# A transformer block on one core: less for GpSimd at three seams, dummy transposes in TensorE's first block, and keys doubled in halves

## The chip, the cores and the metric

The kernel runs on one core of one Trainium2 chip. The metric is the device time of one execution in microseconds. The engines are TensorE (PE), VectorE (DVE), ScalarE (ACT), GpSimd (POOL) and SyncE (SP, which only issues DMAs here). Each works through its own queue in order and waits for others by semaphores.

## The reference

```
x = x + 0.5 * ffn(layernorm(x))            # mixture of 8 experts, 2 chosen per row, and a shared one
x = x + attention_block(layernorm(x))      # attention of 16 heads of 64, Wo, residual, then an MLP
x = x + 0.5 * ffn(layernorm(x))            # the same ffn and weights again
# x: 4 x 1024 x 256, float32
# ffn: scores = sigmoid(x @ gate_W) * route_scale; top 2, weights divided by their sum
#      h_e = gelu(x @ W1_e + b1_e); y_e = h_e @ W2_e + b2_e; sum of gate_e * y_e, plus the shared expert
# attention: q = (ln(x)*s_q + b_q) @ Wq + bq, likewise k and v; p = softmax(q k' / 16 + mask)
```

## The kernel before, in words

The 4096 rows are worked in 8 blocks of 512 (`NB`), the feature dimension of 256 in 2 chunks (`DC`). Every product is split: a float32 operand becomes a rounded high part (mostly ScalarE, names with `_hi`) and a low part that is the difference (mostly VectorE, `_lo`), and three matmuls (`PARTS`) are summed.

`ffn_phase` is built twice; the first time `tail` is true. It prepares weights first: ScalarE rounds the gate weights, w1, w2, b2 and the selection matrix `sel`; VectorE makes the low part of w1, GpSimd that of w2 (L570). Then `over_blocks` runs `body` for each block. In a body the loop variable `e` goes over 9 experts, the shared one first. For each, TensorE computes the hidden layer (`first_layer`, L840) and broadcasts the gate (`gate`, L858), ScalarE applies gelu (L458), VectorE multiplies by the gate (L673), ScalarE rounds (L450), VectorE takes the low part (`lo`, L679), and TensorE adds the second layer two experts behind (`second_layer`, L879). Between these stand, at fixed values of `e`, the steps that prepare the next block: statistics, normalisation, transposes (L807), logits (L817), and the gates (`neg_logits`, `choices`, `gates`), whose transposed form `gst` (`gate_stack`, L668) is what the gate matmuls of the next block need. GpSimd computes powers (reciprocal roots and the exponential of the logits); ScalarE does the exponential in the first block alone.

With `tail`, the body also normalises the finished rows of the block before (`z_stats`, `z_norm`, `zz_stats`, `zn_norm`, transposes to zT), for attention. In blocks 0 and 7 it splits the scaled QKV weights (`qkv_hi`, `qkv_lo`, at the places of `QKV_AT`). The bias of the layer norm has to go through the QKV weights too: for the first `AT_ONCE` groups of 128 columns of Q and K by `first_bias` (L891), for the rest by products and a sum on GpSimd in the last block (`bias_products`, L545 and L548) and matmuls against ones in attention's first four steps (`later_bias`, L905).

`attention_phase` takes two heads at a time ("pair") for 1024 rows; one step `k` is 128 rows of queries of one head: scores (L1538), maximum (L1453), exponential (L1305), division on GpSimd (L1378), eight transposes (L1550), copies, and values (L1574). Before step 0, `FIRST` lists five projections: K, K, Q, Q, V. ScalarE copies each out of PSUM with its bias (`stage`, L1267), GpSimd rounds both heads (`heads_hi`, L1352 and L1353), VectorE takes the low parts (L1428). Each head's K is then copied to the other 64 partitions by DMA (`double_k`, L1152), which the scores of step 0 wait for. The last block's z chain (`rest["z_stats"]` and so on) is worked between these and the first seven steps. The MLP and the second `ffn_phase` follow; the change does not touch what they do.

Of the kernel before, what the change touches and what calls it, by code (L numbers as in the profile page):

```python
# [20 lines left out]
F32 = mybir.dt.float32  # L21
# [103 lines left out]
def ffn_phase(nc, turns, tag, src, dst, w, tail):  # L125
# [8 lines left out]
    AT_ONCE = 2  # L134
# [99 lines left out]
    if tail:  # L234
        names += " gate_in w1_in w2_in zeroed gw_hi w1_hi w2_hi sel gw_lo w1_lo w2_lo b2_hi b2_stack kept"
        names += " z_veps z_bn z_stats z_rs z_rstd z zn zT_ps zT_hi zT_lo zT_out z_out qkv_in v_in summed qs qkv_hi qkv_lo qkv_out bias_ps bias"
    else:
        names += " w1_back w2_back"
# [17 lines left out]


# [10 lines left out]
    def on_sync(sp):  # L268

        def first_loads():  # L270
# [8 lines left out]
            for at, to in ((0, E), (E, 2 * E + 1), (LOW, LOW + NE)):  # L279
                sp.dma_start(b2_in[at:to], w["b2"][0:to - at]).then_inc(s["w2_in"], 16)  # L280
            sp.dma_start(sel_in[:], w["sel"]).then_inc(s["w2_in"], 16)
# [11 lines left out]
        def keep_weights():  # L293
# [4 lines left out]
            sp.wait_ge(s["w2_lo"], 1)  # L298
# [98 lines left out]
    def on_scalar(act):  # L397
# [29 lines left out]

        def xt_hi(i, par):
# [23 lines left out]
        def body(i, par, first, last):  # L452
            for e in range(NE):
# [10 lines left out]
                if e == 2 and not last:  # L464
# [37 lines left out]
    def on_gpsimd(pool):  # L502
# [38 lines left out]
        def bias_products(k):  # L541

            pool.wait_ge(s["qkv_lo"], (k + 1) * DC)
            for c in range(DC):
                o = pool.tensor_scalar(qkv_in[:, k, c], qkv_in[:, k, c], ln[:, k, c, 1:2], 1.0, ALU.mult, ALU.mult)  # L545
            o.then_inc(s["summed"], 1)
            pool.wait_ge(s["summed"], 2 * k + 1)
            pool.tensor_tensor(qkv_in[:, k, 0], qkv_in[:, k, 0], qkv_in[:, k, 1], ALU.add).then_inc(s["summed"], 1)  # L548

        def body(i, par, first, last):  # L550
            if tail and last:
                bias_products(0)
                bias_products(1)
# [8 lines left out]
            if tail and last:  # L562
                bias_products(2)
                pool.wait_ge(s["summed"], 6)
        if tail:
# [3 lines left out]
            pool.wait_ge(s["w2_hi"], 1)  # L569
            pool.tensor_tensor(w2p[:, 1], w2_in[:], w2p[:, 0].bitcast(F32), ALU.subtract).then_inc(s["w2_lo"], 1)  # L570
# [5 lines left out]
    def on_vector(dve):  # L576
# [129 lines left out]

        def zt_lo(i, c, ps):
# [17 lines left out]
        if tail:  # L725
# [12 lines left out]
            gates(0)  # L738
            dve.wait_ge(s["b2_hi"], 1)
# [1377 lines left out]
```

## Time and profile before

| | us |
|---|---|
| median of 3 runs (lowest to highest) | 2468.53 (2466.96 to 2470.21) |
| profiled execution | 2464.61 |
| its span | 2462.8 |
| PE busy in the span | 2404.3 |
| DVE busy | 1866.7 |
| ACT busy | 1680.8 |
| POOL busy | 1529.1 |

The span is the time between the first and the last instruction that the profiler saw; busy PE time counts matmuls in flight and is not PE at its peak. The mean granted clock of TensorE is 0.994 of full speed: only a few short stretches are at half. The chain that ended last is on PE for 81% of the span and on DVE for 8%.

### The profile page before, as it was taken

Reading aid. Unit: us, or ns where it says so; the run is one execution under the profiler, and the core shown is the slowest. Engines: PE = TensorE matmul, PEld = TensorE weight load, DVE = VectorE, ACT = ScalarE, POOL = GpSimd, SP = SyncE. Lnnn points to the kernel's source line nnn. Section 1 sums busy time; section 2 is a strip of 40 time slices with the busy share of each in tenths; the row PEclk is TensorE's granted clock in tenths of the full one; section 3 lists DMA queues with packets and bytes.
Section 4 is the critical chain, followed back from the end, with each engine's and each line's share of the span. In section 5 each row is a group of like instructions: output and inputs, shape, how many; then the busy total and the mean of one; then the engine's idle time right before and its main releaser. Section 6 shows DMA issues by size and latency. Waiting matters only on the chain.

```text
span 2462.8 us, 46531 instructions
## 1 busy us (share of the span) xinstructions
PE 2404.3 (98%) x14504; PEld 2086.9 (85%) x14504; DVE 1866.7 (76%) x3594; ACT 1680.8 (68%) x2913; POOL 1529.1 (62%) x1550
## 2 busy tenths in 40 slices
PE   7999799999999999999999999999999999999999
PEld 6988688888888888888888888888888889988888
DVE  6777777878878787887878878787887865556665
ACT  4554477878778787887878778787787864443333
POOL 2333477777777777777777777777777755542220
PEclk9999999999999999999999999999999999999999
DMA  4522531213222122221213212122221345331111
GB/s 175 199 102 94 171 116 47 87 57 97 72 65 94 43 85 77 85 94 43 85 60 94 84 53 94 43 85 83 79 94 43 108 167 172 119 128 35 48 51 43
DMA packets 127894, 220.15 MB, mean 89 GB/s; under 512 B 6778, under 2 KB 89620, under 8 KB 118932
## 3 DMA queue, kind: packets, MB, share of 16 engines
q1 hardware_dynamic: 127764, 218.78, 27.5%
q8 instruction: 37, 0.61, 0.1%
q14 instruction: 93, 0.76, 0.1%
HBM read 114.95 MB, written 53.48 MB: 68 GB/s over the span
## 4 chain that ended last, share of the span: by engine, by line
PE 81%; DVE 8%; issue 6%; POOL 2%; ACT 2%; DMA 0%; DVEq 0%; SPq 0%; ACTq 0%; POOLq 0%
PE a_ov L1574 19%; PE a_sc L1538 18%; PE a_tr L1550 18%; PE a_pj L1493 7%; PE a_pj L1502 4%; PE g_acc L879 3%; PE g_hid L840 3%; PE f_acc L879 2%; PE f_hid L840 2%; PE m_proj L1976 2%; PE m_hid L2042 1%; DVE f_hp L679 1%; POOL m_zin L1828 1%; PE m_acc L2013 1%; PE f_aux L817 1%
## 5 line engine op out<-in xcount | busy, mean ns | idle before, releaser
L1453 DVE TENSOR_REDUCE a_nmax<-a_sc 128x1 f32<-128x1024 f32 x512 | 626.8, 1224 | 262.4 <-PE a_sc L1538 254.0
L1378 POOL TENSOR_SCALAR a_pr<-a_pr,a_rden 128x1024 f32<-128x1024 f32 x512 | 576.2, 1126 | 258.8 <-DVE a_rden L1458 189.6
L1299 ACT ACTIVATE a_pT<-a_tr 128x512 fp32r<-128x512 f32 x1024 | 559.9, 596 | 209.1 <-PE a_tr L1550 207.6
L1464 DVE TENSOR_TENSOR a_pT<-a_tr,a_pT 128x512 fp32r<-128x512 f32 x1024 | 650.1, 677 | 15.6 <-ACT a_pT L1299 15.6
L1574 PE MATMUL a_ov<-a_pT,a_v_s 128*128 128x512 f32 x2048 | 600.2, 415 | 3.1 <-DVE a_half L1444 2.0
L1305 ACT ACTIVATE a_pr<-a_sc,a_nmax 128x1024 f32<-128x1024 f32 x512 | 573.4, 1120 | 32.5 <-DVE a_nmax L1453 28.9
L1538 PE MATMUL a_sc<-a_k_s,a_q_s 128*128 128x512 f32 x2048 | 555.2, 393 | 6.7 <-DMA a_k_s<-a_k_s 6.7
L1550 PEld LDWEIGHTS a_tr<-f_ident,a_pr 128*128 128x128 f32 x4096 | 473.9, 140 | 89.5 <-DVE a_pT L1464 17.8
L1550 PE MATMUL a_tr<-f_ident,a_pr 128*128 128x128 f32 x4096 | 537.6, 273 | 6.9 <-DVE a_pT L1464 6.9
L1538 PEld LDWEIGHTS a_sc<-a_k_s,a_q_s 128*128 128x128 f32 x2048 | 380.5, 188 | 87.3 <-DMA a_k_s<-a_k_s 6.9
L1574 PEld LDWEIGHTS a_ov<-a_pT,a_v_s 128*128 128x128 f32 x2048 | 347.5, 189 | 54.2 <-issue 4.9
L1493 PE MATMUL a_pj<-a_z_s,a_wqk_s 128*128 128x512 f32 x756 | 193.7, 391 | 2.2 <-issue 2.2
L1493 PEld LDWEIGHTS a_pj<-a_z_s,a_wqk_s 128*128 128x128 f32 x756 | 141.7, 188 | 34.5 <-issue 2.6
L1267 ACT ACTIVATE a_staged<-a_pj,f_bias 128x512 f32<-128x512 f32 x126 | 86.7, 688 | 91.1 <-PE a_pj L1493 68.9
L458 ACT ACTIVATE g_act_out<-g_hid,f_b 128x512 f32<-128x512 f32 x72 | 49.6, 688 | 144.7 <-PE g_hid L840 144.7
L458 ACT ACTIVATE f_act_out<-f_hid,f_b 128x512 f32<-128x512 f32 x72 | 49.3, 684 | 114.9 <-PE f_hid L840 114.9
L879 PEld LDWEIGHTS f_acc<-f_w2p,f_hp 128*128 128x128 f32 x864 | 113.1, 192 | 10.5 <-DVE f_hp L679 5.7
L879 PE MATMUL f_acc<-f_w2p,f_hp 128*128 128x256 f32 x864 | 116.7, 285 | 3.2 <-DVE f_hp L679 2.5
L879 PEld LDWEIGHTS g_acc<-g_w2p,g_hp 128*128 128x128 f32 x864 | 112.1, 191 | 8.4 <-DVE g_hp L679 3.3
L840 PE MATMUL f_hid<-f_xT,f_w1p 128*128 128x512 f32 x432 | 118.6, 412 | 0.0
L879 PE MATMUL g_acc<-g_w2p,g_hp 128*128 128x256 f32 x864 | 115.7, 284 | 1.3 <-DVE g_hp L679 0.9
L840 PE MATMUL g_hid<-g_xT,g_w1p 128*128 128x512 f32 x432 | 113.1, 397 | 0.0
(214 smaller groups left out, 3273.8 us busy)
## 6 DMA issues: line engine op xcount, KB each, us to landing
a_z_s<-zT SPq DMA_DIRECT2D x32, 1024.0 KB, 7.9
a_k_s<-a_k_s SPq DMA_DIRECT2D x64, 512.0 KB, 5.9
a_wqk_s<-w_split SPq DMA_DIRECT2D x64, 256.0 KB, 3.2
a_v_s<-a_v_b SPq DMA_DIRECT2D x16, 1024.0 KB, 4.6
att<-a_ao SPq DMA_DIRECT2D x32, 512.0 KB, 2.9
m_in<-att SPq DMA_DIRECT2D x16, 1024.0 KB, 6.0
a_wv_s<-w_split SPq DMA_DIRECT2D x17, 512.0 KB, 3.8
zT<-f_zT SPq DMA_DIRECT2D x8, 1024.0 KB, 3.9
```

What stands on the lines that cost most here:

```text
L458: act.activation(act_out[:, e % 3], hid[:, (par + e) % 2], ACT.Gelu, bias=b1[:, weights_of(e):weights_of(e) + 1]).then_inc(s["gelu"], 1)
L840: o = pe.matmul(hid[:, (par + e) % 2], w1p[:, a, (c * NE + x) * HID:(c * NE + x + 1) * HID], xT[:, par, c, b], start=(n == 0), stop=(n == 5))
L879: o = pe.matmul(acc[:, t], hp[:, e % 3, a, t * P:(t + 1) * P], w2p[:, b, x * D:(x + 1) * D], start=False, stop=(e == NE - 1 and (a, b) == ...
L1299: act.activation(pT[:, (u // 4) % 2, 0, 4 * part:4 * part + 4, (u % 4) * P:(u % 4 + 1) * P], tr[:, part].rearrange("p (t q) -> p t q", t=4 ...
L1305: act.activation(pr[:, k % NP], sc[:, k % 2], ACT.Exp, bias=nmax[:, k % NP:k % NP + 1], accum_out=den[:, k % NP:k % NP + 1]).then_inc(s["e ...
L1378: pool.tensor_scalar(pr[:, k % NP], pr[:, k % NP], rden[:, k % NP:k % NP + 1], 1.0, ALU.mult, ALU.mult).then_inc(s["normed"], 1)
L1453: dve.tensor_reduce(nmax[:, k % NP:k % NP + 1], sc[:, k % 2], AX.X, ALU.max, negate=True).then_inc(s["negmax"], 1)
L1464: dve.tensor_tensor(to[:, 1], tr[:, part].rearrange("p (t q) -> p t q", t=4), to[:, 0].bitcast(F32), ALU.subtract).then_inc(s["tr_lo"], 1)
L1493: o = pe.matmul(bank[:], wqk_s[:, "QK".index(kind), c, a], z_s[:, c * 2 + b, part], start=(i == 0), stop=(i == 5))
L1538: o = pe.matmul(sc[:, k % 2, kb * BT:(kb + 1) * BT], q_s[:, slot, head, tile * P:(tile + 1) * P], k_s[:, slot, head, a, kb * BT:(kb + 1) * ...
L1550: o = pe.transpose(tr[:, part, j * P:(j + 1) * P], pr[:, (k - LAG) % NP, (4 * part + j) * P:(4 * part + j + 1) * P], ident[:])
L1574: o = pe.matmul(ov[:], v_s[:, vslot, kt, 2 * vhead:2 * vhead + 2] .rearrange("p k f -> p (k f)"), pT[:, blk % 2, a, kt], start=(kt == 0 an ...
```

## The change

- In the first block (`tail` and `first`), TensorE does dummy transposes of the identity into `acc`, which is overwritten later: 20 before the first transposes, 22 after them, 6 after the logits, 10 after `first_bias` and 10 after `gates_up`.
- GpSimd no longer makes w2's low part. VectorE does (`w2_low`), the shared expert's columns at e = 0 and the others at e = 1 of block 0. Its first residual `lo(0, 0)` moves ahead of the loop.
- b2 and sel get a semaphore of their own, and ScalarE rounds them before w2.
- In block 0 the steps that prepare block 1 come two experts later (`later`), `choices` one later.
- `AT_ONCE` goes from 2 to 1.
- GpSimd's bias products and sums go; in the last block, at e = 4, 6 and 7, ScalarE scales one chunk (`bias_product`) and VectorE multiplies and adds (`bias_sum`).
- In attention's five first projections ScalarE writes the second head's high part straight from PSUM, GpSimd only the first head's. K is doubled in two halves, ahead of the stores of zT and of rows on SP. The z chain of the last block starts at steps 1 to 3 instead of before the fourth projection.

The diff, cut to its core:

```diff
-    AT_ONCE = 2
+    AT_ONCE = 1
+    SUMS_AT = {4: 0, 6: 1, 7: 2}
+    def later(first):
+        return 2 if tail and first else 0
...
+        def bias_product(k):
+            act.wait_ge(s["qkv_lo"], (k + 1) * DC)
+            act.activation(qkv_in[:, k, 1], qkv_in[:, k, 1], ACT.Identity, scale=ln[:, k, 1, 1:2]).then_inc(s["scaled"], 1)
...
-                if e == 2 and not last:
+                if e == 2 + later(first) and not last:
                     xt_hi(i + 1, 1 - par)
...
+                if tail and last and e in SUMS_AT:
+                    bias_product(SUMS_AT[e])
...
-            act.wait_ge(s["w2_in"], 80)
-            act.activation(w2p[:, 0], w2_in[:], ACT.Identity).then_inc(s["w2_hi"], 1)
+            act.wait_ge(s["sel_in"], 64)
             act.activation(b2s[:], b2_in[:], ACT.Identity).then_inc(s["b2_hi"], 1)
             act.activation(sel[:], sel_in[:], ACT.Identity).then_inc(s["sel"], 1)
+            act.wait_ge(s["w2_in"], 16)
+            act.activation(w2p[:, 0], w2_in[:], ACT.Identity).then_inc(s["w2_hi"], 1)
             act.wait_ge(s["neg"], 1)
             act.activation(nl[:], nl[:], ACT.Exp).then_inc(s["expneg"], 1)
...
-            if tail and last:
-                bias_products(0)
-                bias_products(1)
...
-            if tail and last:
-                bias_products(2)
-                pool.wait_ge(s["summed"], 6)
...
-            pool.wait_ge(s["w2_hi"], 1)
-            pool.tensor_tensor(w2p[:, 1], w2_in[:], w2p[:, 0].bitcast(F32), ALU.subtract).then_inc(s["w2_lo"], 1)
...
+        def bias_sum(k):
+            dve.wait_ge(s["scaled"], k + 1)
+            dve.scalar_tensor_tensor(out=qkv_in[:, k, 0], in0=qkv_in[:, k, 0], scalar=ln[:, k, 0, 1:2], in1=qkv_in[:, k, 1],
+                                     op0=ALU.mult, op1=ALU.add).then_inc(s["summed"], 1)
+        def w2_low(which):
+            dve.wait_ge(s["w2_hi"], 1)
+            dve.tensor_tensor(w2p[:, 1, which], w2_in[:, which], w2p[:, 0, which].bitcast(F32), ALU.subtract)\
+                .then_inc(s["w2_lo"], 1)
...
             gates(0)
+            lo(0, 0)
...
+                    w2_low(slice((NE - 1) * D, NE * D))
+                if tail and first and e == 1:
+                    w2_low(slice(0, (NE - 1) * D))
                 if not last:
-                    if e == 0:
+                    if e == 0 + later(first):
                         x_stats(i + 1, 1 - par)
...
-                    if e == 7:
+                    if e == 7 + later(first) // 2:
                         choices(i + 1)
...
+        def keep_warm(n):
+            for t in range(n):
+                pe.transpose(acc[:, t % 2, 0:P], ident[:], ident[:])
...
                         first_bias()
+                        keep_warm(10)
                     gates_up(i)
+                    if tail:
+                        keep_warm(10)
...
             pe.wait_ge(s["gate_in"], 64)
+            keep_warm(20)
             transposes(0, xn, s["xn"], s["xT_ps"])
+            keep_warm(22)
             pe.wait_ge(s["gw_lo"], 1)
             logits(0, 0)
+            keep_warm(6)
...
+        for part in range(2):
+            sp.wait_ge(s["first_split"], part + 1)
+            double_first(part)
         rest["store_zT_ahead"]()
         rest["store_rows"]()
-        sp.wait_ge(s["first_split"], 2)
-        double_k(0)
...
+        def second_head_hi(kind, part, n):
+            _, hi, _ = parts_of(kind, part, n % 2, 0)
+            act.activation(hi[1], bank_of(n, True)[rows_of_head(1)], ACT.Identity, bias=bias_of(rows_of_head(1), 0, "QK".index(kind)))\
+                .then_inc(s["head1_hi"], 1)
         for n, (kind, part) in enumerate(FIRST):
             stage(kind, n, n % 2, 0, True)
+            if kind != "V":
+                second_head_hi(kind, part, n)
...
-                if first and k == 1:
+                if first and k == 2:
                     rest["z_norm"]()
...
-                heads_hi(kind, part, n, n % 2, 0, n)
+                (x0, _), hi, _ = parts_of(kind, part, n % 2, 0)
+                pool.wait_ge(s["staged"], n + 1)
+                pool.tensor_scalar(hi[0], x0, 1.0, 1.0, ALU.mult, ALU.mult).then_inc(s["head0_hi"], 1)
...
-                if first and k in (0, 3):
+                if first and k in (1, 3):
                     rest["z_rstds"](k // 3)
...
-            if n == 3:
-                rest["z_stats"]()
...
+                if first and k == 1:
+                    rest["z_stats"]()
-                if first and k == 2:
+                if first and k == 3:
                     rest["zz_stats"]()
```

## Rows read from the trace of the kernel before

**Rows 1.** The page's head.
```profile
span 2462.8 us, 46531 instructions
```

**Rows 2.** Chain of waits, 0 to 110 us: start us, us, what.
```profile
13.46 3.56 PE f_aux L817 x16
...
17.83 3.55 DVE f_sg L630
...
26.84 0.70 DVE f_gst L668
...
28.38 2.56 PE f_hid L840 x6
...
42.56 1.39 PE f_hid L840 x6
...
58.74 1.28 DVE f_qkv_s L703
```

**Rows 3.** Timeline, 0 to 72 us: start us, us, engine, line, operation, [idle before <-releaser].
```profile
6.01 0.22 ACT L482 ACTIVATE f_gwp<-f_gw_in 128x16 fp32r<-128x16 f32 x1 [3.87 <-DMA f_rsc<-in_rscale]
...
10.01 1.94 PE L807 MATMUL f_aux<-f_ident,f_xn 128*128 128x128 f32 x8 [10.01 <-DVE f_xn L597]
...
14.04 2.12 ACT L488 ACTIVATE f_w2p<-f_w_in 128x2304 fp32r<-128x2304 f32 x1 [1.46 <-DMA f_w_in<-in_w]
...
16.25 5.09 POOL L570 TENSOR_TENSOR f_w2p<-f_w_in,f_w2p 128x2304 fp32r<-128x2304 f32 x1 [7.80 <-ACT f_w2p L488]
...
60.53 0.68 DVE L668 CAST f_gst<-f_aux 128x512 fp32r<-128x512 f32 x1
```

**Rows 4.** Timeline, 212 to 275 us.
```profile
222.98 0.68 DVE L668 CAST f_gst<-f_aux 128x512 fp32r<-128x512 f32 x1
...
254.88 2.34 POOL L548 TENSOR_TENSOR f_qkv_in<-f_qkv_in 128x1024 f32<-128x1024 f32 x1
254.91 2.35 DVE L653 TENSOR_TENSOR f_ga<-f_iota,f_idf 128x32 f32<-128x32 f32 x1
...
259.19 1.12 PE L827 MATMUL f_aux<-f_ident,f_gpad 128*128 128x128 f32 x4 [4.73 <-DVE f_zT L709]
...
260.35 0.69 DVE L668 CAST f_gst<-f_aux 128x512 fp32r<-128x512 f32 x1
```

**Rows 5.** Windows: us, busy (instructions) of each engine, PEclk, DMA share, GB/s.
```profile
26.00:28.00 2.00, 1.22 (x5) 0.81 (x4) 1.18 (x6) 0.00 (x0) 0.00 (x0) 0.50 0.00 0
...
2188.00:2189.00 1.00, 1.00 (x11) 1.00 (x10) 0.24 (x1) 0.87 (x2) 0.00 (x0) 1.00 0.00 0
...
2193.00:2194.00 1.00, 1.00 (x4) 0.79 (x3) 0.65 (x1) 0.11 (x1) 1.00 (x1) 0.53 0.00 0
```

**Rows 6.** Timeline of the last block, 253 to 285 us.
```profile
254.00 1.14 ACT L425 ACTIVATE f_qkv_s<-f_qkv_in,f_ln 128x1024 fp32r<-128x1024 f32 x1
...
277.00 2.08 ACT L401 ACTIVATE f_zz<-f_res,f_zshift,f_zrs 128x256 f32<-128x256 f32 x4 [2.32 <-POOL f_zshift L534]
...
281.03 1.70 PE L879 MATMUL f_acc<-f_w2p,f_hp 128*128 128x256 f32 x12 [1.28 <-DVE f_hp L679]
```

**Rows 7.** Timeline of the step into attention, 275 to 345 us.
```profile
297.55 1.12 POOL L1353 TENSOR_SCALAR a_k_s<-a_staged 64x512 fp32r<-64x512 f32 x1
...
308.67 2.08 PE L1538 MATMUL a_sc<-a_k_s,a_q_s 128*128 128x512 f32 x4 [6.68 <-DMA a_k_s<-a_k_s]
...
312.78 1.17 PE L905 MATMUL a_ov<-f_iota,f_qkv_in 128*128 128x1 f32 x10
```

**Rows 8.** Chain of waits, 225 to 372 us.
```profile
302.41 6.22 DMA a_k_s<-a_k_s
```

**Rows 9.** The page's DMA issues: KB each, us to landing.
```profile
a_wqk_s<-w_split SPq DMA_DIRECT2D x64, 256.0 KB, 3.2
```

**Rows 10.** TensorE's timeline, 2176 to 2216 us.
```profile
2188.37 1.04 PE L2027 MATMUL m_hT_ps<-f_ident,m_hn 128*128 128x128 f32 x8
2190.11 1.95 PE L817 MATMUL g_aux<-f_gwp,g_xT 128*128 128x16 f32 x16 [0.70 <-DVE g_xT L604]
```

More of the change, by code:

```diff
@@ L279, in first_loads @@
             for at, to in ((0, E), (E, 2 * E + 1), (LOW, LOW + NE)):
[L280 to L281 removed]
+                sp.dma_start(b2_in[at:to], w["b2"][0:to - at]).then_inc(s["sel_in"], 16)
+            sp.dma_start(sel_in[:], w["sel"]).then_inc(s["sel_in"], 16)
             sp.dma_start(w2_in[:], w["w2"]).then_inc(s["w2_in"], 16)
@@ L757, in body @@
                     result(i - 1)
-                if e > 0:
+                if e > 0 and not (tail and first and e == 1):
                     lo(i, e - 1)
-                elif not first:
+                elif e == 0 and not first:
                     lo(i - 1, NE - 1)
@@ L794, in body @@
                         qkv_lo(k, c)
+                if tail and last and e in SUMS_AT:
+                    bias_sum(SUMS_AT[e])
         over_blocks(dve, body)
@@ L874, in second_layer @@
                               start=(t % 2 == 0), stop=False, skip_group_check=True)
+            if first and tail and e == 1:
+                pe.wait_ge(s["w2_lo"], 2)
             pe.wait_ge(s["h_lo"], i * NE + e + 1)
@@ L898, in later_bias @@
             if part == 0:
-                pe.wait_ge(s["summed"], 6)
+                pe.wait_ge(s["summed"], 3)
             ones = iota[:, 1:2]
             groups = [(k, g) for k, a, b in LATER_BIAS for g in range(a, b)]
-            n = len(groups) // parts
-            for at in range(part * n, part * n + n):
+            n = -(-len(groups) // parts)
+            for at in range(part * n, min(part * n + n, len(groups))):
                 k, g = groups[at]
@@ L926, in body @@
                 if not last:
-                    if e == 2:
+                    if e == 2 + later(first):
                         transposes(i + 1, xn, s["xn"], s["xT_ps"])
-                    if e == 3:
+                    if e == 3 + later(first):
                         logits(i + 1, 1 - par)
@@ L1153, in double_k, with double_first @@
                     .then_inc(s["k_dup"], 16)
+        def double_first(part):
+            cols = slice(part * BT, part * BT + BT)
+            for head, (a, b) in enumerate(((0, HD), (HD, 0))):
+                sp.dma_start(k_s[b:b + HD, 0, head, :, cols].bitcast(F32), k_s[a:a + HD, 0, head, :, cols].bitcast(F32))\
+                    .then_inc(s["k_dup"], 16)
         def move_v():
@@ L1285, in body @@
                         act.wait_ge(f["z_out"], NB * 16 + 16)
-                        act.wait_ge(f["bias"], 4)
                     if blk % 4 == 0 and not first:
@@ L1308, in body @@
                         kind, _, n, slot = piece_at(it, k)
+                        if first and k == 5:
+                            act.wait_ge(f["bias"], 4)
                         stage(kind, n, slot, (2 * it + 1 + k // STEPS) % PAIRS, False)
```

26 lines of the change are left out of this document (11 added, 15 removed).

## The prediction

> **What bounds the kernel now.** I read the page's head first: the span is 2462.8 us of the profiled execution's 2464.61 [rows 1], so 1.8 us lie outside it; TensorE is busy in nearly all of it, and the attention loop that fills most of it is not touched. So only the pauses in the first 345 us can move the time. I then read the chain of waits there and the timelines beside it. In the first block the chain goes through TensorE's 16 small logits matmuls (3.56 us), then VectorE's gate work, where one 128x32 operation takes 3.55 us [rows 2]. The timeline shows GpSimd's residual of w2 from 16.25 to 21.34, and the slow operation ends just after it [rows 3]; the same kind of operation elsewhere is over in 0.2 us, so some 3.4 us are GpSimd in VectorE's way. In the last block VectorE's copy of the gates (f_gst) comes 37.37 us after that of the block before, where the five intervals ahead took 32.49 each ((222.98-60.53)/5) [rows 3, 4]: 4.9 us late. There a 128x32 operation took 2.35 us beside GpSimd's sum over the bias products, and TensorE stood 4.73 us [rows 4]. Third, attention starts only after a pause of 6.68 us, in which the doubled K is copied by DMA [rows 7, 8].
>
> **The first block.** Removed: GpSimd's w2 residual. VectorE does it in two pieces, after the gates. That takes 3.4 us off VectorE's chain ahead of f_gst.
> Added on TensorE: 20+22+6 dummy transposes around the first transposes and logits, 10+10 around the first gates_up. Their price depends on the clock. Eight transposes take 1.94 us in the first block [rows 3] and 1.04 us at 2188.37 [rows 10]; less the tail of the last one (0.42 and 0.27) that is 0.22 us each at the low level (1.2 GHz) and 0.11 us at the high one (2.4 GHz). Six 512-column matmuls take 2.56 us low and 1.39 us high [rows 2]; the granted clock is 0.50 at 26 to 28 us and 1.00 at 2188 [rows 5].
> The first 20 can begin when the small loads are in (6.01, where ScalarE begins) and take 4.4 us low: to 10.4, where the real transposes began at 10.01 [rows 3]. That is 0 to 0.4 us late; ScalarE is rounding w1 then, so I take 0. If dummies raise the clock as dense work does, it is high by about 12 us. The 22 then end near 14.2 where the logits began at 13.46: 0.7 us late, but the logits themselves take about 1.8 instead of 3.56 (16 x 0.11 with a tail). The negated logits come 1.0 us earlier. ScalarE has finished rounding w2 at 16.16 (14.04+2.12) [rows 3], just before they are there, so its exponential does not wait. The words of the change put this exponential ahead of two roundings; in the diff it stays behind all of them, and only b2 and sel go ahead of w2, in the idle time before w2 lands. Worth 0 either way.
> Without the 3.4 us stall the gates are ready 4.4 us earlier (21.3). TensorE gets there at 16.6 (logits, 6 dummies) + 2.8 (12 matmuls) + 0.9 (bias, 8 instructions instead of 16) + 1.1 (10 dummies) = 21.4: level. f_gst is then at 23.1 instead of 27.5; it is late by one residual (0.7) and the b2 one (0.4), which now stand before it on VectorE. So 4.4 - 0.7 + the 0.6 that gates_up is faster at the high clock: about 4.4 us at this point (26.84+0.70 [rows 2]).
> Then the block's own order. w2's second piece is 2048 of 2304 columns, about 2.3 us on VectorE; stats, norm, transposes and logits of the next block come two experts later, choices one later and directly ahead of the gates. TensorE first runs ahead of before by two experts (6.1 us), and gives it back at the end: choices start when the last expert's residual is done (49.0), then 2.2 + 2.2 + two qkv residuals of 1.28 [rows 2] + 1.3 put f_gst of the next block at 57.1 to its end, where it was 61.2 [rows 3]. What is late next is thus VectorE, not TensorE. Gain carried on: **4.0 us**, bounds 2.5 and 6.
>
> **The last block.** GpSimd's products and sums are gone, so f_gst comes at the usual interval: +4.9 us. The clock also does not fall behind a 4.73 us pause, where matmuls were half as fast for some 5 us; on the way to the first second-layer group I read 2.0 us from that. Together **+6.9**; bounds 5.5 and 7.5.
> In their place come three ScalarE scalings (1.14 each by its 128x1024 activation [rows 6]) and three VectorE multiply-adds (1.28 each by the qkv residual [rows 2]), at experts 4, 6 and 7. The one at expert 4 stands on ScalarE behind the normalisation of z, which waited for GpSimd until 277.00 and ran 2.08 [rows 6]. The multiply-add is at the head of VectorE's queue and waits for it: 279.1 + 1.14 + 1.3 = 281.6, and behind it stand gating and residual of two experts, 0.7 + 0.7, so TensorE's group that began at 281.03 after 1.28 us of waiting [rows 6] begins at 283.0: 1.9 late. At expert 7 the same pattern behind the second normalisation adds another 0.5, although the stalls by GpSimd there are gone. **-2.4**; bounds -0.5 (if another order of arrivals hides two) and -4. The pause before that group becomes 3.2 us. The pauses of 4.73 and 6.68 us brought the low clock [rows 4, 7]: the four score matmuls behind the second took 2.08 us; I take one fall in most executions, for three to four us at half speed: **-1.3**, bounds 0 and -2.
>
> **Into attention.** Each K and Q piece had both heads' high parts made by GpSimd, 1.12 us for one while VectorE works [rows 7]. Now ScalarE makes one straight from PSUM (in its idle time) and GpSimd the other. VectorE no longer waits for the second; K's two halves are split at about 298.8 and 300.7 (each step 0.7 on each of the two engines), where before the last issue of the copy was only out at 302.41 [rows 8]; each half is doubled as soon as it is split, ahead of two stores on the sync queue. The transfer after the last issue took 6.22 us for 512 KB [rows 8]; 256 KB pieces of the same queue take 3.2 in the median [rows 9]. From an issue at 301.3, with 3.2 to 5 us: 304.6 to 306.3, I take 305.6, against 308.67 [rows 7]: +3.0. The pause shrinks to about 3.6 us and the clock may still fall; before, the low level reached 3.6 us into the work, and now it could reach further: -0.7. Two more bias groups are made here, 4 instructions at 0.117 (1.17 per 10 [rows 7]): -0.5. The stats of z go from ahead of the last Q piece to step 1, the rest of that chain one step later; VectorE has 2 us gaps in these steps, ScalarE's 2.08 us normalisation now stands before the first transposed probabilities: 0, bounds -1.5 and +1.5. **+1.8** in all, bounds -0.5 and +5.
>
> **Sum.** 4.0 + 6.9 - 2.4 - 1.3 + 1.8 = 9.0 us. Against the profiled 2464.61 that is 2455.6; that execution lay 3.9 below the median of 2468.53, so for the median I say **2459.5**.
>
> **The rivals.**
> *Dummies that don't wake the clock.* For: no stretch of this trace is filled by transposes and followed by a rise; and a busy TensorE is not enough, since at 2193 the clock fell with no longer pause than 0.7 us behind it, after 16-column matmuls [rows 5, 10]. Against: the transposes just before those [rows 10] were passed with the clock at 1.00, which then stood for four more us [rows 5]. The price: the 22 low take 4.9 us from 12.3, so the logits end at 20.8; 6 dummies, 12 matmuls at 0.45, the bias and 10 dummies at 0.11 to 0.22 put gates_up at 29.3 to 31.5, and behind it 10 more: the first gate matmul is 3.5 to 7.5 us later than before (27.5). The block's own order takes the same 0.4 as above and a low stretch behind it 1. The first block then loses 5 to 8.8 instead of winning 4.0. Total 0.0 on the mild end (2468.5) and, if the clock stays low through the whole first stage, 3.8 us slower: **2472**. It decides at the 22 dummies ahead of the logits: the clock must be high before about 14 us.
> The Trainium skill says in "TensorE: Matmul & The Clock Gate", Part 4, PE-mode transpose, that transposes do not engage the full clock because they don't count as busy in the same way; that is this rival. By that rule the time would be the 2468.5 to 2472 just worked out, and by the rows of eight transposes passed at full clock it would be mine.
> *The last block keeps nothing.* ScalarE and VectorE queues are in order, and three waits are put at VectorE's head. If these cost the 4 us of the bound and a fall of the clock with each of two pauses (another 2), the sum is 9.0 - 1.6 - 2 = 5.4: **2463**. For it: at expert 4 ScalarE has 4.5 us of work (gelu and rounding 1.3, the normalisation 2.08, the scaling 1.14), and a block leaves 32.49 / 9 = 3.6 per expert.
> *Everything on the good side.* No fall of the clock at either seam and attention's ramp a step faster: 9.0 + 1.3 + 2.5 = 12.8: **2455.7**. Shorter pauses than those that brought a fall speak for it.
> *The words, not the deed.* The keys' copy may be bound by its start-up, not its size, so that halving gives nothing and only the 1 us earlier split counts: -2 of the sum, **2461.5**; within my range.
>
> **How the numbers follow.** My forecast 0.42, the good side 0.17, the last block 0.13, the unhalved copy 0.10, the sleeping clock 0.18 (two thirds of it near 2468, one third slower). The range to hold 8 in 10: from 2452 (between the good case and its bounds) to 2468. About 0.2% (5 us) is what a measurement of this kernel can tell: faster than 2463.6 is all of the first three but half of the last-block case, and the copy: 0.74; the sleeping clock and the rest within: 0.20; beyond 2473.5, its far end or a wait I haven't seen: 0.06.
>
> **What would show it.** The granted clock high before 14 us and no low stretch at 25 to 32 us; VectorE's L630 operation of the first block at 0.2 us; first f_gst near 23, second near 56.5, then equal intervals of 32.5 through the last block; a TensorE wait of about 3 us at expert 4 of the last block, released by VectorE behind the multiply-add; the first scores about 3 us after V's projection. It is wrong if the logits of the first block start at 17, or if the gains at the seams come back as waits on ScalarE in attention's first seven steps.

## The result: 0.2 to 0.4% faster, in executions of two kinds

The changed kernel was timed twice, each time beside the kernel before on the same chip.

| | changed, us | before, us | ratio, 95% interval |
|---|---|---|---|
| first, 8 executions | 2456.37 (2454.3 to 2464.42) | 2468.80 | 0.9957 [0.9947, 0.9967] |
| again, 11 executions | 2462.39 (2455.01 to 2465.5) | 2467.23 | 0.9980 [0.9971, 0.9990] |
| all 19 | median 2460.97 | | |

The two intervals do not meet. The reason lies in the executions: 8 of the 19 had a mean TensorE clock of 0.996 or more and a median of 2456.1 us, the other 11 lay below that (0.992 to 0.994) and had 2462.9, from 2459.4 to 2465.5. The first time there were six of the quick sort and two of the other, the second time two and nine. Of 81 executions of the kernel before, timed beside the second timing and the experiments, only one had a mean clock of 0.996; their median is 2467.1. So the change gains 11 us in one sort of execution and 4 in the other. One execution of each sort has a trace. Below, the two traces differ by one stretch of low clock where attention begins; of the other executions only time and mean clock are known.

### The profile after, of a quick execution

It took 2457.1 us with this span (page's head); before it was 2464.61 with [rows 1]:

```profile
span 2454.2 us, 46643 instructions
```

The timeline (start us, us, engine, line, operation, [idle before <-releaser]):

```profile
9.86 1.04 PE L822 MATMUL f_aux<-f_ident,f_xn 128*128 128x128 f32 x8
10.73 2.56 PE L904 MATMUL f_acc<-f_ident 128*128 128x128 f32 x22
13.45 1.92 PE L832 MATMUL f_aux<-f_gwp,f_xT 128*128 128x16 f32 x16 [0.15 <-DVE f_xT L601]
...
16.75 0.18 DVE L627 TENSOR_SCALAR f_sg<-f_nl 128x32 f32<-128x32 f32 x1 [0.66 <-ACT f_nl L506]
...
22.27 0.69 DVE L665 CAST f_gst<-f_aux 128x512 fp32r<-128x512 f32 x1
...
52.78 0.66 PE L842 MATMUL f_aux<-f_ident,f_gpad 128*128 128x128 f32 x4 [1.99 <-DVE f_gpad L661]
...
55.63 0.68 DVE L665 CAST f_gst<-f_aux 128x512 fp32r<-128x512 f32 x1
...
89.73 0.68 DVE L665 CAST f_gst<-f_aux 128x512 fp32r<-128x512 f32 x1
...
252.19 0.68 DVE L665 CAST f_gst<-f_aux 128x512 fp32r<-128x512 f32 x1
...
266.22 2.08 ACT L407 ACTIVATE f_zz<-f_res,f_zshift,f_zrs 128x256 f32<-128x256 f32 x4 [2.01 <-POOL f_zshift L548]
268.20 1.13 ACT L437 ACTIVATE f_qkv_in<-f_qkv_in,f_ln 128x1024 f32<-128x1024 f32 x1
269.37 1.28 DVE L707 SCALAR_TENSOR_TENSOR f_qkv_in<-f_qkv_in,f_ln 128x1024 f32<-128x1024 f32 x1 [4.36 <-ACT f_qkv_in L437]
271.91 2.38 PE L896 MATMUL f_acc<-f_w2p,f_hp 128*128 128x256 f32 x12 [2.63 <-DVE f_hp L676]
...
283.35 3.50 PE L896 MATMUL f_acc<-f_w2p,f_hp 128*128 128x256 f32 x24 [1.24 <-DVE f_hp L676]
...
286.69 1.55 PE L1541 MATMUL a_pj<-a_z_s,a_wqk_s 128*128 128x512 f32 x6
293.23 1.66 PE L1550 MATMUL a_pj<-a_wv_s,a_z_s 128*128 128x256 f32 x12 [0.27 <-ACT a_q_s L1309]
298.27 1.19 PE L1586 MATMUL a_sc<-a_k_s,a_q_s 128*128 128x512 f32 x4 [3.38 <-DMA a_k_s<-a_k_s]
...
313.74 1.40 DVE L576 BATCH_NORM_STATS2 f_zst<-f_zz 128x6 f32<-128x256 f32 x4
...
317.58 1.16 PE L1598 MATMUL a_tr<-f_ident,a_pr 128*128 128x128 f32 x8 [2.12 <-DVE a_pT L1509]
...
327.55 1.16 PE L1622 MATMUL a_ov<-a_pT,a_v_s 128*128 128x512 f32 x4 [0.63 <-DVE f_zT L718]
```

What to see, from the top. Eight transposes take 1.04 us, not the 1.94 of [rows 3], although nothing but twenty dummy transposes (5.61 to 10.0) stands ahead of them, and the logits take 1.92, not the 3.56 of [rows 2]. L627, the operation that took 3.55 in [rows 2], takes 0.18. The gates' copy (f_gst) comes at 22.27. In the last block it comes at the usual interval; the pause of [4.73] in [rows 4] is gone, and [2.63] at 271.91 is the new one, at the end of the row of waits ScalarE L407, ScalarE L437, VectorE L707. A second one, of 1.24, stands at 283.35. The pause before the scores is 3.38, where [rows 7] had 6.68. Behind it, at 317.58, TensorE waits 2.12 for VectorE.

The windows (us, busy and instructions of PE, PEld, DVE, ACT, POOL, then PEclk, DMA share, GB/s) show the two low stretches of that trace before attention (54 to 61 and 272 to 276), one behind each of the pauses of 1.99 and 2.63. That attention begins at 1.00 is what sets this execution apart from the slower one traced below:

```profile
55.00:60.00 5.00, 3.84 (x15) 3.40 (x15) 3.64 (x12) 1.21 (x2) 1.26 (x2) 0.50 0.87 367
...
273.00:276.00 3.00, 3.00 (x12) 2.61 (x11) 2.84 (x8) 0.02 (x1) 1.95 (x3) 0.50 1.00 356
...
300.00:305.00 5.00, 5.00 (x42) 4.83 (x41) 2.69 (x5) 2.24 (x4) 0.95 (x3) 1.00 0.69 185
```

And the last copy of K in the chain of waits, against [rows 8]:

```profile
293.76 4.46 DMA a_k_s<-a_k_s
```

### The profile page after: what moved, and what is told of

Same layout as the page of the kernel before. It is cut to its first block, busy times and chain, and to the rows that moved or that the text cites. A ratio compares the mean times of both kernels' runs of the same rounds, so it can differ in the third digit from the quotient of the medians.

```text
span 2454.2 us, 46643 instructions
## 1 busy us (share of the span) xinstructions
PE 2405.0 (98%) x14568; PEld 2087.9 (85%) x14568; DVE 1862.3 (76%) x3599; ACT 1686.6 (69%) x2920; POOL 1505.2 (61%) x1536
## 4 chain that ended last, share of the span: by engine, by line
PE 81%; DVE 8%; issue 6%; POOL 2%; ACT 2%; DMA 1%; SPq 0%; DVEq 0%; ACTq 0%; POOLq 0%
PE a_ov L1622 19%; PE a_sc L1586 18%; PE a_tr L1598 18%; PE a_pj L1541 7%; PE a_pj L1550 4%; PE g_acc L896 3%; PE g_hid L855 3%; PE f_acc L896 3%; PE f_hid L855 2%; PE m_proj L2025 1%; POOL m_zin L1877 1%; PE m_hid L2091 1%; DVE f_hp L676 1%; DVE g_hp L676 1%; PE g_aux L832 1%
```

## The experiments

Each has 5 to 12 executions; "quick" are those with a mean clock of 0.996 or more. They ran on three chips, each beside the kernel before, and the ratio is against that: e1 to e4 (2467.15 for before), e6 to e9 (2466.58), and e5, e10, e11 with the second timing of the changed kernel (2467.23). So only those last three ran on the same chip as the second timing of the changed kernel; whether a chip shifts the share of quick executions was not tested.

| kernel | median us | ratio, interval | quick: n, median | others: n, median |
|---|---|---|---|---|
| changed (both times) | 2460.97 | see above | 8, 2456.1 | 11, 2462.9 |
| e1 no dummies | 2464.24 | 0.9995 [0.9986, 1.0003] | 2, 2458.6 | 10, 2465.1 |
| e7 first 48 only | 2462.75 | 0.9985 [0.9975, 0.9995] | 2, 2455.7 | 9, 2464.3 |
| e9 before + dummies | 2466.44 | 1.0005 [0.9995, 1.0015] | 1, 2464.0 | 10, 2466.8 |
| e2 sums on GpSimd | 2462.46 | 0.9983 [0.9972, 0.9994] | 6, 2459.1 | 6, 2467.7 |
| e3 old seam | 2462.20 | 0.9983 [0.9971, 0.9994] | 1, 2458.1 | 10, 2463.1 |
| e11 one copy | 2462.37 | 0.9976 [0.9968, 0.9985] | 2, 2459.2 | 9, 2463.5 |
| e5 exponential first | 2459.25 | 0.9967 [0.9955, 0.9980] | 4, 2457.9 | 2, 2464.2 |
| e6 pauses filled | 2457.83 | 0.9974 [0.9964, 0.9985] | 8, 2457.0 | 4, 2464.1 |
| e4 scalings first | 2457.88 | 0.9965 [0.9952, 0.9978] | 2, 2453.1 | 3, 2459.5 |
| e8 = e4 + e6 | 2458.52 | 0.9967 [0.9954, 0.9980] | 2, 2453.4 | 4, 2459.1 |
| e10 = e8 + seam filled + e5 | **2452.27** | **0.9936 [0.9923, 0.9949]** | 5, 2452.3 | none |

### The changed kernel again, and what the slower executions are

> The changed kernel itself once more, beside the kernel before on the same chip, so that the versions above have a base measured the same way. Its first eight executions fell into six of 2454 to 2457 us and two of 2462 to 2464. Theory (the variants without some dummies are slower by the median because more of their executions have low-clock stretches): most executions again at 2454 to 2458, median 2456.5, ratio 0.9957. Rival (eight executions were a lucky draw): the median is 2459 to 2461, ratio 0.997 to 0.998, and the dummies are worth 4 us instead of 8.

The rival of a lucky draw held: the ratio is at the edge of its 0.997 to 0.998, and the median 1.4 us above its range. Its profiled execution (2461.93 us) is one of the slower sort, and its windows at the start of attention show what sets it apart; columns as above:

```profile
300.00:305.00 5.00, 5.00 (x22) 4.71 (x22) 0.35 (x1) 1.69 (x3) 0.77 (x2) 0.50 0.56 148
...
315.00:320.00 5.00, 5.00 (x23) 4.51 (x22) 3.04 (x6) 4.05 (x8) 2.47 (x3) 0.55 0.31 105
```

TensorE is busy in all of 300 to 320 and gets half the clock. Its timeline:

```profile
297.70 1.19 PE L1586 MATMUL a_sc<-a_k_s,a_q_s 128*128 128x512 f32 x4 [3.37 <-DMA a_k_s<-a_k_s]
...
301.01 2.55 PE L927 MATMUL a_ov<-f_iota,f_qkv_in 128*128 128x1 f32 x12
...
334.33 1.17 PE L1622 MATMUL a_ov<-a_pT,a_v_s 128*128 128x512 f32 x4 [0.63 <-DVE f_zT L718]
```

After the same pause (3.37 here, 3.38 there) the first scores to the first product with V take 36.63 us here and 29.28 in the quick execution: 7.35 us. The spans of the two differ by 5.8 (the slower one was 0.6 ahead at the first scores and 1.0 quicker behind that product), the medians of the two sorts by 6.8. The other traces with K doubled as in the changed kernel agree in the main: quick executions of e1 and e7 have no low stretch there, a slower one of e5 has one from 298 to 320. The sorts are not clean, though: quick executions of e4, e6 and e8 have two short falls there.

### What the dummies do

e1 takes away all 68, e7 the last 20, and e9 puts all 68 into the kernel before.

```diff
-            for t in range(n):            # e1, in keep_warm
+            for t in range(0):
...
-                        keep_warm(10)     # e7: ahead of and behind gates_up(i)
...
+            keep_warm(20)                 # e9, in the kernel before; likewise 22, 6, 10, 10
             transposes(0, xn, s["xn"], s["xT_ps"])
```

> The changed kernel without its 68 dummy transposes, all else kept. Theory (they hold TensorE's clock high): the logits of the first block take 3.5 us again, the 12 first hidden matmuls about 5.4, the clock is low in part of 20 to 32 us, f_gst of the first block ends near 24.5 instead of 22.96, and the second one comes 1.5 to 4 us later; median 2.5 to 4.5 us above that of the changed kernel. Rival (the first block's gain is GpSimd out of VectorE's way alone, the dummies only fill pauses): f_gst within 0.5 us and the same median within 1 us.

> The changed kernel without the last 20 dummies (10 ahead of and 10 behind the first gates_up); the first 48 stay. Without all 68 the median was 2464.2. Theory (the 48 raise the clock ahead of the logits, and the work behind them keeps it): f_gst of the first block at 22.3 to 22.7, no low stretch before 30, median 2457 to 2458. Rival (the 20 hold the clock across the wait for VectorE's gates): the clock falls between 20 and 32 us, the median is 2460 to 2463.

> The kernel before with the 68 dummies alone. Theory (the dummies' worth is the clock of the first stage, in either kernel): logits in 1.9 us instead of 3.6, and fewer low stretches behind, some 5 us less: median 2462, ratio 0.998. Rival (before, VectorE and GpSimd end the first block, so that a faster TensorE buys nothing there): f_gst of the first block at 26 to 26.5 instead of 26.84, later ones the same or up to 1 us later, since 20 of the dummies stand in TensorE's way; median 2466 to 2468, ratio 0.9995 to 1.0005.

The first three f_gst in the timeline of e1:

```profile
23.79 0.69 DVE L665 CAST f_gst<-f_aux 128x512 fp32r<-128x512 f32 x1
...
57.16 0.69 DVE L665 CAST f_gst<-f_aux 128x512 fp32r<-128x512 f32 x1
...
89.68 0.68 DVE L665 CAST f_gst<-f_aux 128x512 fp32r<-128x512 f32 x1
```

The first two in the timeline of e7:

```profile
22.19 0.69 DVE L665 CAST f_gst<-f_aux 128x512 fp32r<-128x512 f32 x1
...
57.12 0.68 DVE L665 CAST f_gst<-f_aux 128x512 fp32r<-128x512 f32 x1
```

And the first block in the timeline of e9:

```profile
13.80 1.92 PE L817 MATMUL f_aux<-f_gwp,f_xT 128*128 128x16 f32 x16
...
16.31 5.13 POOL L570 TENSOR_TENSOR f_w2p<-f_w_in,f_w2p 128x2304 fp32r<-128x2304 f32 x1 [7.98 <-ACT f_w2p L488]
17.72 3.77 DVE L630 TENSOR_SCALAR f_sg<-f_nl 128x32 f32<-128x32 f32 x1 [1.27 <-ACT f_nl L492]
...
26.94 0.69 DVE L668 CAST f_gst<-f_aux 128x512 fp32r<-128x512 f32 x1 [0.76 <-PE f_aux L827]
```

Without any, the first f_gst is 1.5 us later (23.79 against 22.27) and the second too. With the first 48 the first is as early (22.19), but in the wait for the gates the clock falls from about 23 to 27 us and the second is 1.5 later all the same: it is the last 20 that carry the gain to the second f_gst. At the third nothing is left of it. It comes at 89.68 in e1, 89.63 in e7 and 89.73 in the changed kernel, whose low stretch from 54 to 61 takes the 1.5 back; e1 has a shorter one there (54 to 58), e7 none. Where the changed first block runs without that stretch, in the traces of e3, e4 and e11, the third f_gst comes at 87.8 to 88.3. So by the traces the dummies are worth 0 to 1.5 us, by what the clock does behind them. By the medians e1 is 3.3 us slower than all 19 of the changed kernel and 1.9 slower than its second timing. e1's interval meets that of the second timing but not that of the first, so a larger worth, through fewer slow executions, stays open.

In the kernel before, the dummies bring the short logits too (1.92), and nothing comes of it: VectorE's 3.77 beside GpSimd's 5.13 still ends the chain, f_gst is at 26.94 against 26.84. So the rivals of e7 (by its mechanism, though its median does not differ from the changed kernel's second one) and of e9 held. Most of the first block's gain is there without any dummy: the third f_gst is at 93.03 before and at 89.68 in e1, 3.35 us. That it comes from taking w2's low part off GpSimd is argued: the operation that took 3.55 beside it takes 0.18. But the later steps, the earlier b2 and sel and the fewer bias groups came with it, and no run gives that part alone back to GpSimd.

### The last block

e2 gives the sums over the bias products back to GpSimd; e4 only turns the order on ScalarE.

```diff
+                if tail and last and e in SUMS_AT:      # e4: up here,
+                    bias_product(SUMS_AT[e])
                 if e == 4 and tail and not first:
                     z_norm(i - 1)
 ...
-                if tail and last and e in SUMS_AT:      # not behind it
-                    bias_product(SUMS_AT[e])
```

> The changed kernel with the bias products and sums of the last block back on GpSimd. Theory: the gates ahead of the last block are held up by 4.9 us again (interval of f_gst 37.4 instead of 32.5) with a low clock behind them, while the 1.3 us wait at expert 4 and the low stretch behind it go: 4 to 5 us slower than the changed kernel. Rival (the last block keeps nothing, since ScalarE and VectorE pay on the path what GpSimd cost): within 1.5 us of the changed kernel.

> The changed kernel with ScalarE's scaling put ahead of the normalisation of z at expert 4 (and likewise at expert 7). Theory (the stall at expert 4 of the last block is ScalarE's order): the scaling fits into the 2.0 us in which ScalarE waits for GpSimd, the multiply-add is done before, TensorE's wait there shrinks from 2.6 to about 1.3 us and with it, in most executions, the low clock behind it: 1.3 to 3 us faster. Rival (GpSimd's root and ScalarE's normalisation set the chain anyway): no difference beyond 0.5 us.

e2's timeline has the old row of [rows 4] again, VectorE beside GpSimd:

```profile
251.06 2.34 POOL L560 TENSOR_TENSOR f_qkv_in<-f_qkv_in 128x1024 f32<-128x1024 f32 x1
251.09 2.35 DVE L663 TENSOR_TENSOR f_ga<-f_iota,f_idf 128x32 f32<-128x32 f32 x1
...
256.52 0.69 DVE L678 CAST f_gst<-f_aux 128x512 fp32r<-128x512 f32 x1
```

The interval is 37.4 us again (219.12 to 256.52), and K's projection comes 4.15 us later than in the changed kernel. Over all executions the two medians are only 1.5 us apart and the intervals meet, as the rival would have it; but e2 had six quick executions of twelve, the changed kernel eight of 19. Quick against quick it is 3.0 us more, others against others 4.8, and the trace has the theory's marks: the long interval, a low clock from 254 to 262, the later projection. e4's timeline:

```profile
262.69 1.14 ACT L437 ACTIVATE f_qkv_in<-f_qkv_in,f_ln 128x1024 f32<-128x1024 f32 x1
263.86 1.28 DVE L707 SCALAR_TENSOR_TENSOR f_qkv_in<-f_qkv_in,f_ln 128x1024 f32<-128x1024 f32 x1 [0.27 <-ACT f_qkv_in L437]
269.27 1.70 PE L896 MATMUL f_acc<-f_w2p,f_hp 128*128 128x256 f32 x12 [1.41 <-DVE f_hp L676]
...
282.09 1.55 PE L1541 MATMUL a_pj<-a_z_s,a_wqk_s 128*128 128x512 f32 x6
```

VectorE waits 0.27 instead of 4.36 for the scaling, TensorE 1.41 instead of 2.63, the clock stays up, and from f_gst (250.77) to K's projection it is 31.32 us, against 34.50: 3.2 us. In each sort of execution (two and three) e4 is 3.0 to 3.4 us quicker than the changed kernel, as its theory said, though with five executions its interval meets both of that kernel's.

### The seam into attention

e3 puts the whole attention stage back as it was before; e11 only makes the copy of K one pair of 512 KB transfers again.

```diff
-        for part in range(2):                   # e11
-            sp.wait_ge(s["first_split"], part + 1)
-            double_first(part)
+        sp.wait_ge(s["first_split"], 2)
+        double_k(0)
```

> The changed kernel with the whole attention phase as before: GpSimd rounds both heads, K is doubled at once behind two stores, the z chain starts earlier. Theory: scores begin about 2.8 us later after V's projection, the clock is low behind the pause, and the ramp gives 1 to 2 us back because the z chain is ahead again: 1.5 to 3 us slower. Rival (the copy is bound by its start-up, only the split's 1 us counts): 0 to 1 us.

> The changed kernel with K's first slot doubled in two transfers of 512 KB after both halves are split, instead of four of 256 KB. Theory (the last copy's size counts, 4.5 us in the changed kernel and 6.2 us in the one before): the first scores come 1.5 to 2 us later behind V's projection, the pause ahead of them is 5 us instead of 3.4, and the clock falls for longer; 2 to 3 us slower than the changed kernel. Rival (the copy is bound by its start-up, or by what else the queues carry): the pause is 3.4 to 3.9 us and the time is the same.

e11's timeline:

```profile
291.17 1.67 PE L1549 MATMUL a_pj<-a_wv_s,a_z_s 128*128 128x256 f32 x12 [0.29 <-ACT a_q_s L1308]
298.54 2.07 PE L1585 MATMUL a_sc<-a_k_s,a_q_s 128*128 128x512 f32 x4 [5.70 <-DMA a_k_s<-a_k_s]
```

Its chain of waits (start us, us, what):

```profile
291.66 6.83 DMA a_k_s<-a_k_s
```

From V's projection to the first scores it is 8.34 us before and in e3, 7.37 in e11, 5.04 in the changed kernel. So halving the copies gives 2.3 us, and the earlier split with the place ahead of the two stores 1.0. The copy is not bound by its start-up alone. The medians do not show it (e3 and e11 are 1.2 and 1.4 us slower than all 19 of the changed kernel, and the intervals meet that of its second timing): e3 and e11 both had the long low stretch in their profiled executions (294 to 322 and 297 to 321), and so has the changed kernel in the slower of its two.

Behind the scores the new order of attention's first steps costs time. e2 shows it, since it has the new attention phase and, like the kernel before, a low clock only in the first 3.4 to 4 us of work from the scores on:

```profile
302.56 2.07 PE L1597 MATMUL a_sc<-a_k_s,a_q_s 128*128 128x512 f32 x4 [3.38 <-DMA a_k_s<-a_k_s]
...
333.29 1.17 PE L1633 MATMUL a_ov<-a_pT,a_v_s 128*128 128x512 f32 x4 [0.63 <-DVE f_zT L731]
```

From the first scores to the first product with V it is 30.73 us here and was 28.56 before (308.67 to 337.23): 2.2 us more, of which the four more bias instructions are some 0.5. The rest fits the wait at 317.58 in the changed kernel's timeline above. There TensorE waits 2.12 us for the low part of the transposed probabilities, and VectorE has taken the statistics of zz (from 313.74, one step later than before) ahead of it; before, the same wait was 0.27. It is 2.12 in the traces of e1, e2, e6 and e7 too, 0.93 in e4 and e8 and 0.27 in e10, which have a low stretch in these steps, and 0.26 where the clock was low for 20 us (the slower changed one, e5, e11). No run moves the z chain alone, so that it is the cause is argued.

### Filling the pauses, and a better kernel

```diff
+                    if tail and last and e == 6:        # e6, in TensorE's body
+                        fill(aux[:, 0], 20)
...
+                    if tail and first and e == 8:
+                        fill(aux[:, 1], 14)
...
+                    if first and k == 0:                # e10, ahead of the wait for K's copy
+                        for t in range(26):
+                            pe.transpose(tr[:, 0, (t % 4) * P:(t % 4 + 1) * P], ident[:], ident[:])
```

> The changed kernel with 14 more dummy transposes behind expert 8 of the first block (where TensorE stood 1.99 us and the clock was low from 54.4 to 61.0) and 20 ahead of expert 4's second layer in the last block (a wait of 2.63 us, low from 272.8 to 276). Theory (a pause of TensorE brings the low stretch, so filling the pause keeps the clock high): both low stretches are gone, the interval from the second to the third f_gst is 32.5 instead of 33.4, projection K0 comes 18.3 behind the last block's f_gst instead of 19.7 to its end's matmuls, in all 2.5 us less: median 2454. Rival (the low stretches come of themselves, whatever stands in the pauses): they are there again and the time stays at 2456.4. Second rival (dummies end behind the release): f_gst or expert 4 is 0.5 us later and the median is 2456 to 2457.

> ScalarE's scalings ahead of the two normalisations of z, together with the 14 and 20 dummies in the pauses. The scalings alone gave 2457.9 in the median of 5 and 2451.4 in the profiled run. Theory (a wait shortened by 1.2 us and two pauses filled, each by itself): 1.2 + 2.5 us less than the changed kernel, median 2452.5 to 2453. Rival (the shorter pause is worth nothing once the clock is held, or the 20 dummies now stand in the way, since only 1.4 us of pause are left for 2.2 us of them): no better than the dummies alone, 2454 to 2456.

> The changed kernel with ScalarE's first exponential ahead of the rounding of w2 (as the words of the change have it). In the changed kernel this exponential began 0.35 us after the negated logits were there. Theory (it is on the way to the gates, and w2's low part is behind them): f_gst of the first block 0.3 us earlier, w2 rounded 1 us later with 1 us to spare ahead of VectorE's second piece; 0 to 0.3 us faster, the same within the measurement. Rival (the table load between exponential and rounding, or w2's later rounding, delays the first second layer at expert 3): the first block loses 1 to 2 us, 2457.5 to 2458.5.

> Scalings ahead of the normalisations, the 14 and 20 dummies in the pauses, the exponential ahead of w2's rounding, and 26 dummies more in TensorE's pause ahead of the first scores, where 3.4 us of waiting for the copy of K stand. Without the last two: 2458.5 (6 executions). Theory (the low stretch at the start of attention is what is left): scores in 1.2 us and no clock below 1.00 between 295 and 320, 1.5 to 2.5 us less in the median, and 0.3 us from the exponential: 2455 to 2456. Rival (the clock falls by other causes there, in the bias matmuls of one column or the pauses of attention's ramp): low stretches between 300 and 320 as before, no gain: 2458 to 2459.

In e6's profile both early low stretches are gone and the second f_gst is followed by the third after 32.51 us (55.72, 88.23), not 34.1. That the filling of the first pause does this is not shown. Of the nine traces that leave it at 1.98 or 1.99 us, four have a low stretch behind it (both of the changed kernel, e1, e2) and five have none (e3, e4, e5, e7, e11). e4's f_gst, without the filling:

```profile
88.27 0.69 DVE L665 CAST f_gst<-f_aux 128x512 fp32r<-128x512 f32 x1
```

At expert 4 of the last block the traces speak for it: all seven with a pause of 2.63 or 2.64 there have a low stretch behind it, the five with a shorter or filled one (e2, e4, e6, e8, e10) have none. But little comes of the clock. From f_gst to K's projection it is 34.21 us in e6 and 34.50 in the changed kernel, because TensorE then waits for VectorE at the place where the changed kernel waits 1.24:

```profile
281.55 3.50 PE L896 MATMUL f_acc<-f_w2p,f_hp 128*128 128x256 f32 x24 [2.46 <-DVE f_hp L676]
```

Low stretches also appear at 297 to 301 and 317 to 321, and e6's median is 3.8 us above the theory's 2454. e8 is no better than e4, and its 2458.5 is above both the theory and the rival. e5 loses 0.8 us at the first f_gst, and its timeline shows how:

```profile
16.26 0.23 ACT L504 ACTIVATE f_nl<-f_nl 128x32 f32<-128x32 f32 x1 [2.41 <-DVE f_nl L610]
...
18.52 1.28 ACT L507 ACT_TABLE_LOAD   x1
19.81 1.52 ACT L469 ACTIVATE f_act_out<-f_hid,f_b 128x512 f32<-128x512 f32 x2
...
21.88 0.69 DVE L676 TENSOR_TENSOR f_hp<-f_act_out,f_hp 128x512 fp32r<-128x512 f32 x1 [0.86 <-ACT f_hp L461]
...
23.06 0.69 DVE L665 CAST f_gst<-f_aux 128x512 fp32r<-128x512 f32 x1
```

The exponential waits for VectorE 2.41 us in which w2 could have been rounded; the rounding and the table load then put the first gelu at 19.81 instead of 17.95. VectorE has its first residual (L676) ahead of the copy to f_gst and waits 0.86 for ScalarE, and f_gst is 0.8 later. A part of that may come from a low clock at 15 to 19 us, which only this trace has; e10, with the same order and no such stretch, has f_gst at 22.76, 0.5 later than the changed kernel.

e10 adds 26 dummies at the seam. Its timeline:

```profile
290.69 3.00 PE L1580 MATMUL a_tr<-f_ident 128*128 128x128 f32 x26
294.26 1.19 PE L1598 MATMUL a_sc<-a_k_s,a_q_s 128*128 128x512 f32 x4 [0.57 <-DMA a_k_s<-a_k_s]
```

All its five executions had a mean clock of 0.997 or more, where of the changed kernel's eleven on the same chip two reached 0.996. It is 6.3 us quicker than e8, although it carries e5's loss; e8 ran on another chip. The scores do not come earlier behind V's projection (5.08 us, 5.04 in the changed kernel), so the gain is in the clock. It came out better than either text had it, 2.7 us below the theory's range, and yet the theory's mark failed: 303 to 311 us are low, the only low stretch of its first 345 us. It beats the kernel before by 0.64%, and each of its five executions (2449.38 to 2453.23) was quicker than all 19 of the changed kernel. What it does not rule out, with one trace, is a fall later in attention's first steps: e8 had one at 305 to 308 as well.

## Why the prediction came out right

The forecast was 2459.5 us in 2452 to 2468. The first timing gave 2456.4, the second 2462.4, the median of all 19 is 2461.0. The forecast gain of 9.0 stands against 12.4 the first time and 4.8 the second. For the profiled quick execution the prediction's sum was 2455.6 and the measurement 2457.1, of which 1.1 is more time outside the span (2.9 against 1.8). By its steps, from starts in the two profiled executions of the changed kernel against the rows of before:

| step | predicted us | quick execution us | slower execution us |
|---|---|---|---|
| first block (third f_gst 93.03, now 89.73; slower 89.25) | 4.0 | 3.3 | 3.8 |
| last block (interval 37.37, now 32.47; then f_gst to K's projection 33.96, now 34.50; slower 32.47 and 34.49) | 6.9 - 2.4 - 1.3 = 3.2 | 4.9 - 0.5 = 4.4 | 4.4 |
| K's projection to the first product with V (42.92, now 40.86; slower 48.20) | 1.8 | 2.1 | -5.3 |
| the rest of the kernel | 0 | -1.1 | -0.1 |
| sum, of the span (up to 0.1 of rounding) | 9.0 | 8.6 | 2.8 |

So the steps agree with the quick execution. In the slower one the two blocks hold and the seam's -5.3 lies outside its bounds of -0.5 and +5.

**First block.** The dummies do raise the clock; f_gst was forecast to end at 23.1 and ends at 22.96. The logits were not 0.7 us late at all. w2 landed later than before and the exponential waited some 0.35 us for its rounding, where I had said it would not wait. The second f_gst was forecast to end at 57.1 (the terms given add up to 57.3) and ends at 56.31, bound by VectorE as said. What I missed stands behind it: a low stretch from 54 to 61, behind a pause of 1.99 us, takes 1.6 us and breaks the equal intervals that the prediction named as a sign. Five traces with the same pause do not have it, so it is not the pause alone. With it, nothing is left at the third f_gst of what the dummies gained (89.73, and 89.68 without them in e1).

**The sleeping clock** (0.18) is refuted by 1.04 us for eight transposes and 2.56 for 22 more, behind nothing but transposes, in e5, e7, e9 and e10 likewise (1.04 to 1.10, and 2.56 to 2.57); without dummies, in e1, the eight take 1.94 again. That rival would have made 2468.5 to 2472. The Trainium skill says in "TensorE: Matmul & The Clock Gate", Part 4, PE-mode transpose, that transposes do not engage the full clock. For the float32 transposes of these traces that does not hold, and the measurement decides.

**Last block.** The row of waits at expert 4 stood as written: normalisation, scaling, multiply-add, then a TensorE wait, of 2.63 us instead of 3.2, and one low stretch. e4 proves the cause. The sizes were off, and in part against each other. From f_gst to that group of TensorE it was 20.68 us before and is 18.50 in e4: 2.2 by the clock, where 2.0 stood. It is 19.72 in the changed kernel, so ScalarE's order costs 1.2 there, not 1.9. From the group to K's projection it was 13.28 and is 14.78: 1.5 lost, where 0.5 for expert 7 and 1.3 for the clock stood. e6 has no low stretch and still takes 14.48. So the fall of the clock was worth 0.3, not 1.3, and the order at expert 7, with its wait of 1.24, some 1.2 instead of 0.5. In all 0.5 was lost where 1.7 (2.0 - 2.4 - 1.3) were expected.

**Seam.** Predicted were +3.0 for the copy, -0.7 for the clock, -0.5 for the bias groups and 0 for the z chain. Measured are +3.3 to the scores, less 0.5 ahead of V's projection (its distance from K's went from 6.02 to 6.54), which the prediction did not have. Behind the scores the new order costs 2.2 with the bias groups (e2 against before), so what stood at 0 with bounds of 1.5 costs some 1.7. The clock then gives 1.5 back in the quick execution (29.28 against e2's 30.73) and takes 5.9 in the slower one (36.63). That 2.1 came out where 1.8 was forecast is luck: two errors of opposite sign. The rival of the unhalved copy falls by e11.

**What the prediction did not have** is that the same kernel has two prices at the seam. It gave "the low level could reach further" 0.7 us. In the traced slower execution it costs 7.35 against the quick one, and 11 of 19 executions have that lower mean clock. Of the kernel before 80 of 81 executions lie below 0.996, so its one trace did not show the choice. The forecast is near the overall median because it lies between the two sorts, which no step of it foresaw. That is luck too.

**Open.** Why the clock stays low for 20 us in some executions with TensorE busy throughout, and 3 to 7 or not at all in others after the same pause. The stretch holds the one-column bias matmuls; moving those was not tried.

## What to carry to other kernels

Fill a wait of TensorE that stands just ahead of many small matmuls: there a fall of the clock can cost twice the wait (7.35 us for 3.38), and with the wait filled none of e10's five executions was of the slower sort. Filling a wait behind which another engine is next in line gives little (0.3 us in e6). In queues that are served in order, put the short operation that another engine's queue head waits for ahead of the long one that waits itself (3 us here for two lines). Before you credit a change of 0.2%, look at the mean clock of each execution: the same kernel gave 0.9957 and 0.9980.

## What the hardware showed unexpectedly

- Dummy transposes alone, from 5.61 us on, were enough for the high level by about 9.9 us: eight transposes took 1.04 us there, and 1.94 without the dummies (e1).
- The same pause of 1.99 us was followed by a low stretch in four traces and by none in five.
- The first rows of a trace can show PEclk 1.00 where operations still take low-level times: before at 10.01 [rows 3]. There only durations tell.
- A fully busy TensorE stayed at half the clock for 20 us (300 to 320), after a pause of 3.4 us that in another execution brought no fall.
- A 128x32 operation of VectorE that takes 0.18 us alone ended only with GpSimd's beside it: 3.77 us beside 5.13 (e9), 2.35 beside 2.34 (e2).
- A copy within SBUF from partitions to partitions took 6.2 (before) to 6.8 us (e11) from the last issue at 512 KB and 4.5 at 256 KB.
